# Attention of the second layer with its slots in another order on four engines: the fourth turned group is copied early, and each output is turned back and scaled within its own slot

## The reference, cut to what matters

```python
    def _L1_xattn_ref(hidden_states_query, hidden_states_key, attention_mask, Wq, bq, Wk, bk, Wv, bv):
        ...
        NUM_HEADS = 16
        HEAD_DIM = HIDDEN // NUM_HEADS
        ...
        q = _split_heads(hidden_states_query @ Wq.T + bq)
        k = _split_heads(hidden_states_key @ Wk.T + bk)
        v = _split_heads(hidden_states_key @ Wv.T + bv)
        scale = 1.0 / np.sqrt(HEAD_DIM)
        scores = jnp.einsum('bhqd,bhkd->bhqk', q * scale, k)
        scores = scores + ((1.0 - attention_mask) * -10000.0)[:, None, :, :]
        probs = jax.nn.softmax(scores, axis=-1)
        ctx = jnp.einsum('bhqk,bhkd->bhqd', probs, v)
        b, h, lq, d = ctx.shape
        return ctx.transpose(0, 2, 1, 3).reshape(b, lq, h * d)
```

## Time and profile before

| | |
|---|---|
| median of 3 runs | 851.43 us (850.89 to 852.59) |
| profiled execution, its time | 849.4 us |
| its span | 847.6 us |
| granted TensorE clock, mean | 0.984 |
| PE busy | 776.9 us (92%) |
| DVE busy | 506.0 us (60%) |
| ACT busy | 399.9 us (47%) |
| POOL busy | 227.0 us (27%) |
| the 15 slots from the first ACT copy of slot 1 to that of slot 16 | 489.22 to 614.81, 125.59 us |
| first `hidden` of the feed-forward that the attention no longer holds up (unit 1) | DVE at 632.29 |

### The profile page before, as it was taken

One profiled execution on the slowest core, in us unless ns is written; L12 is line 12 of the kernel. 1 busy time (PEld: TensorE's weight loads), 2 busy tenths in 40 slices (PEclk: granted clock), 3 DMA queues, 4 the chain that ended last, 5 costly groups with the idle time before them and its releaser, 6 DMA issues.

```text
span 847.6 us, 15310 instructions
## 1 busy us (share of the span) xinstructions
PE 776.9 (92%) x5406; PEld 625.7 (74%) x5406; DVE 506.0 (60%) x1159; ACT 399.9 (47%) x817; POOL 227.0 (27%) x208
## 2 busy tenths in 40 slices
PE   8667899999999999999999789996789999999997
PEld 7466487788887888888887455654568878888886
DVE  5588875465583333343342897978766665756644
ACT  5598554244462222222223688778635344243222
POOL 0079210046501332232234166764300000000000
PEclk9989999999999999999999999999999999999999
DMA  8478740033242334443332600102004023050140
GB/s 303 143 263 300 279 169 1 1 126 125 99 164 69 63 63 70 78 79 63 68 45 31 221 13 27 63 2 75 2 2 102 1 51 76 1 126 0 27 100 26
DMA packets 37512, 74.47 MB, mean 88 GB/s; under 512 B 4448, under 2 KB 25568, under 8 KB 35680
## 3 DMA queue, kind: packets, MB, share of 16 engines
q1 hardware_dynamic: 30288, 64.16, 24.0%
q0 software_dynamic: 7152, 9.34, 6.4%
HBM read 59.76 MB, written 19.01 MB: 93 GB/s over the span
## 4 chain that ended last, share of the span: by engine, by line
PE 54%; DVE 16%; ACT 8%; DVEq 4%; issue 4%; DMA 2%; ACTq 0%; POOLq 0%; SPq 0%
PE t_y_ps L2281 8%; PE f_y L1775 4%; PE a_turned L999 3%; PE a_score L977 2%; ACT a_hhi L1165 2%; PE t_gate L2251 2%; PE a_score L978 2%; PE a_score L979 2%; PE t_up L2262 2%; PE t_up L2263 2%; PE t_up L2261 2%; PE t_gate L2252 2%; PE t_gate L2253 2%; PE a_proj L876 2%; PE t_h_turned L2270 2%
## 5 line engine op out<-in xcount | busy, mean ns | idle before, releaser
L2221 POOL DMA_INDIRECT sums<-t_y,t_dest x39 | 60.9, 1561 | 168.4 <-DMA sums<-t_y,t_dest 81.3
L2316 ACT CAST t_xT_hi<-t_x_turned 128x256 fp32r<-128x256 f32 x39 | 14.5, 372 | 139.2 <-PE t_x_turned L2242 139.2
L2281 PE MATMUL t_y_ps<-W,t_hidT 128*128 x312 | 73.8, 379 | 0.8 <-ACT t_hidT L2326 0.8
L1165 ACT CAST a_hhi<-a_hid 128x512 fp32r<-128x512 f32 x48 | 29.8, 620 | 87.5 <-DVEq L1450 85.9
L2281 PEld LDWEIGHTS t_y_ps<-W,t_hidT 128*128 128x128 f32 x312 | 59.1, 190 | 10.5 <-issue 1.0
L1452 DVE TENSOR_TENSOR a_hlo<-a_hid,a_hhi 128x512 fp32r<-128x512 f32 x48 | 33.2, 693 | 35.1 <-ACT a_hhi L1165 35.1
L1154 ACT ACTIVATE a_act_g<-a_score 128x512 f32<-128x512 f32 x48 | 28.6, 596 | 46.4 <-PE a_score L979 45.9
L2345 DVE TENSOR_TENSOR t_hid<-t_act_g,t_up 128x512 f32<-128x512 f32 x39 | 28.5, 731 | 35.9 <-ACT t_act_g L2321 32.6
L832 POOL TENSOR_TENSOR a_sc<-a_sc,a_nmx 128x512 f32<-128x512 f32 x32 | 33.3, 1042 | 55.8 <-DVE a_nmx L1298 55.8
L1114 ACT ACTIVATE a_pr<-a_sc,a_nmx 128x128 f32<-128x128 f32 x128 | 40.8, 390 | 14.3 <-DVE a_nmx L1298 13.5
L2356 DVE TENSOR_SCALAR t_y<-t_y_ps,t_dest 128x256 f32<-128x256 f32 x39 | 18.9, 484 | 38.3 <-PE t_y_ps L2281 38.3
(11 more groups left out here) (426 smaller groups left out, 2287.8 us busy)
## 6 DMA issues: line engine op xcount, KB each, us to landing
W<-in_w_dram SPq DMA_DIRECT2D x9, 1536.0 KB, 8.1
a_cb<-comb_rows SPq DMA_DIRECT2D x16, 512.0 KB, 8.2
W<-m_rows SPq DMA_DIRECT2D x14, 512.0 KB, 4.9
slot_tokens<-in_blank_rows_dram SPq DMA_DIRECT2D x1, 5031.0 KB, 20.5
t_x<-slot_tokens SPq DMA_DIRECT2D x39, 129.0 KB, 3.0
a_raw<-in_w_dram SPq DMA_DIRECT2D x3, 1536.0 KB, 6.7
X<-in_x_dram SPq DMA_DIRECT2D x4, 512.0 KB, 6.1
ctxT_all<-in_ctxT_dram SPq DMA_DIRECT2D x4, 512.0 KB, 8.7
```

Of the source, the lines that this page charges most:

```text
L1165: act.copy(hhi[u % 2][:], hid[u % 2]).then_inc(hhi_ready, 1)
L2221: pool.indirect_dma_start(sum_dram, bass.IndirectOffsetOnAxis(ap=dest[p][:, 0:1].bitcast(U32), axis=0), y[p][:], None, compute_op=ALU.add) ...
L2281: last = pe.matmul(y_ps[p][:, 0:D], hidT[p][:, h], W[:, ds(e, 1), at:at + D], start=(h == 0), stop=(h == HT - 1))
```

## The change

It moves instructions and makes none new. `soft` is cut into `penalise` and `maxima`, so that something can stand between them. On PE, `turn_back(s-1)` comes behind `scores(s+1)` of the same slot instead of between the second and third `turn` of the next; `values(s-1, 3)` comes ahead of `scores(s+1)` instead of behind; the early projection comes behind `values(s-1, 1)` instead of ahead of `values(s-1, 0)`. On DVE, the copy of group 3 stands between the two halves of the scores, and `finish` stands at the slot's end, for sequence `s-1`; a late projection is copied one slot later, ahead of that copy. On ACT, `keep_out` stands between the two pairs of exponentials. On POOL, the addition to `X` stands behind the second `centre`.

```diff
@@ gpsimd
-            for s in range(B + 2):
+            for s in range(B + 1):
                 if s < B:
                     centre(s, 1)
-                if s >= 2:
-                    pool.wait_ge(o_ready, s - 1)
-                    pool.tensor_tensor(X[:, s - 2, :], X[:, s - 2, :], o_sb[s % 2][:], ALU.add).then_inc(added, 1)
                 pieces(s, 0)
                 if s < B:
                     centre(s, 3)
+                if s >= 1:
+                    pool.wait_ge(o_ready, s)
+                    pool.tensor_tensor(X[:, s - 1, :], X[:, s - 1, :], o_sb[(s - 1) % 2][:], ALU.add).then_inc(added, 1)
                 pieces(s, 1)
                 if s in (6, 11):
                     penalties(2 + (s == 11))
@@ tensor
                 if past:
                     turn(s - 1, 0)
                     turn(s - 1, 1)
-                if s >= 2:
-                    turn_back(s - 2)
-                if past:
                     turn(s - 1, 2)
                 if s == B:
                     gate_up(0)
-                if s == B + 1:
-                    break
-                if early:
-                    project(early)
                 if past:
                     values(s - 1, 0)
                     values(s - 1, 2)
                     turn(s - 1, 3)
                     values(s - 1, 1)
+                if early:
+                    project(early)
+                if s == B:
+                    gate_up(1)
+                if past:
+                    values(s - 1, 3)
                 if s + 1 < B:
                     scores(s + 1)
+                if 1 <= s < B:
+                    turn_back(s - 1)
                 if late:
                     project(late)
...
-                if past:
-                    values(s - 1, 3)
-                if s == B:
-                    gate_up(1)
...
                 down(u)
+                if u == 0:
+                    turn_back(B - 1)
@@ scalar
-                elif s == PREP0 + 1:
-                    normalise(0)
                 if s < B:
                     exps(s, 0)
                     exps(s, 1)
+                if s == PREP0 + 1:
+                    normalise(0)
                 keep(early)
+                if 1 <= s < B:
+                    keep_out(s - 1)
                 if s < B:
                     exps(s, 2)
                     exps(s, 3)
...
-                if s >= 1:
-                    keep_out(s - 1)
+                    keep_out(B - 1)
@@ vector
                 if s < B:
-                    soft(s, 0)
-                if s >= 2:
-                    finish(s - 2)
+                    penalise(s, 0)
+                    maxima(s, 0)
+                if past:
+                    keep(parts_of(s - 1)[1])
                 if s in (1, CH + 1):
                     normalise2(s // CH + 2)
-                if s < B:
-                    soft(s, 1)
-                keep(early)
-                if s == B:
-                    route_groups(0)
                 if past:
                     keep_turned(s - 1, 3)
                 if s == B - 1:
                     route_logits(0)
-                keep(late)
+                if s < B:
+                    penalise(s, 1)
+                if s in (PREP0 + 2, PREP0 + 3):
+                    keep_lo(0, s - PREP0 - 2)
+                if s < B:
+                    maxima(s, 1)
+                keep(early)
+                if 1 <= s < B:
+                    finish(s - 1)
...
-                elif s in (PREP0 + 1, PREP0 + 2):
-                    keep_lo(0, s - PREP0 - 1)
                 elif s == B:
+                    route_groups(0)
                     hidden(0)
+                    finish(B - 1)
                     route_second(0)
```

More of the change, by code:

```diff
@@ L1009, in _ @@
                 project(part)
-            for s in range(B + 2):
+            for s in range(B + 1):
                 early, late = parts_of(s)
-                past = 1 <= s <= B
+                past = s >= 1
                 if past:
@@ L1286, in normalise2, with penalise @@
                 last.then_inc(rows_dve, 1)
-            def soft(s, half):
+            def penalise(s, half):
                 c, j = s // CH, s % CH
@@ L1297, in soft, with maxima @@
                 dve.drain()
+            def maxima(s, half):
+                part = sc[s % 2][:, 2 * half:2 * half + 2].rearrange("p r i t -> p (r i) t")
                 dve.tensor_reduce(nmx[s % 2][:, 2 * half:2 * half + 2].rearrange("p r i -> p (r i)"), part, AX.X, ALU.max,
```

## The result

The changed kernel took 871.21 us (median of four runs, 867.34 to 874.5), against 851.17 us for the kernel before beside it (850.89 to 852.59). The ratio is 1.023, 95% interval 1.0181 to 1.028: slower by 20.0 us. The forecast was +14.2 us. The same program, timed again on another chip, gave 869.06 us against 850.58: ratio 1.0224 (1.0197 to 1.0251), +18.5 us. Direction and mechanism were right; the size was 4 to 6 us short. That it is slower is clear of the noise; whether by more than 2% is not, since both intervals hold 1.02.

A forecast was written before the change was run, and what follows sets the result against it. The prediction took a ring through four engines, closed by DVE's copy of group 3, to set slot lengths: +11.5 us in slots, +2.7 in the tail, 14.2 on 851.4, giving 865.6 us; 8-in-10 range 856 to 872.

The forecast's parts named there:

- What bounds the kernel: Attention before the change: PE near its limit only in early slots; a plain slot set by a 7.0 us cross-engine ring.
- the ring: Attention slots: DVE's copy of group 3 waits for PE's fourth turn, delaying penalty, maximum and exponentials; plain slot 8.0 us.
- The late slots: Slots 10 to 15: about break even, 54.7 us against 53.6, since their 2 us idle stretches go.
- 137.1: Slots 1 to 15: forecast slot lengths summed, in us, against 125.6 before, +11.5.
- I take +2.7: Tail, slot 16 to hidden(1): route_groups behind the copy and a wait at finish(15) delay hidden(1) by 2.7 us.
- K: Start of ACT's first copy in a slot, from which times count; the tail's hidden(0) was forecast 8.65 us after it.
- I carry the shift to the end at its full size: Behind the tail: PE busy nearly throughout in the same order, so the delay of hidden(1) reaches the end whole.
- the rival at 870 to 876 us: Early slots also drop to 1.2 GHz, about 1.4 us a slot in six slots, up to 8 us more; chance 13%.
- the ring's own, 858 to 870: Whole kernel: time range in us if the slots run as summed, 865.6 likeliest; chance 70%.
- the first rival: Slots: the copy of group 3 does not bind, 6.9 us a slot, about 844 us in all; chance 7%.
- PE does not hide it: Denies the rival that slots with projections stay at 8.7 us, PE covering late projections; 851 to 854 us, chance 10%.

The follow-up runs named there:

- e1: Changed kernel with the fourth turn ahead of the values of group 2 on PE; 865.59 us against 852.35 for the kernel before, ratio 1.0127.
- e6: Changed kernel with DVE's copy of group 3 moved behind the second penalty, still ahead of its maximum; 864.29 us against 869.06 for the plain changed kernel.
- e5: Changed kernel with extra identity transposes on PE filling idle stretches in slots 1 to 3 and 10 to 16; 868.2 us against 869.06 without them.
- e9: The kernel before, unchanged, profiled and timed again; 855.73 us against 854.12 for the same program in the same set, ratio 1.0023.
- e8: The changed kernel, unchanged, timed and profiled again on another chip; 869.06 us against 850.58 for the kernel before.
- e4: Changed kernel with DVE's order in slot 16 put back as before (route_groups ahead of the copy, finish(15) behind the routing); 868.93 us against 852.35, ratio 1.0163.
- e3: Kernel before with only DVE's copy of group 3 moved between the halves of the scores, behind finish(s-2); 888.52 us in one run.

## Why the prediction came out as it did

**What bounds the kernel, and the ring: right.** A plain slot took 7.95 (forecast 8.0), slots 2 and 3 took 8.46 and 8.47 (8.5), slot 4 took 9.68 (9.8), slot 5 took 10.17 (10.4), slots 6 and 7 took 8.48 (8.5), slots 8 and 9 as 4 and 5, slot 10 took 8.02 (8.0). e1 took wait from L1307, e6 put work into it, and slots 1 to 3 became shorter both times.

**The late slots: right within 1.2 us in all at the full clock.** In e5 slots 10 to 15 took 55.91 against 54.7 forecast; slot 11 was the term most off, 9.95 against 9.4. That the sum of all 15 slots comes within 0.3 us is better than its parts. The comparison with before has a flaw that could not be resolved: 137.1 is a sum at the full clock, 125.6 a measurement with a granted clock of 0.94 in its late slots, and neither profile of the kernel before had the full clock there. Slot 12 is the long one, as forecast: POOL's penalties stand behind the addition, which waits for `finish`. POOL, DVE and PE of the changed kernel there:

```profile
590.43 2.04 POOL L800 TENSOR_SCALAR a_pen<-a_pen 128x512 f32<-128x512 f32 x1
...
592.57 1.22 DVE L1295 TENSOR_TENSOR a_sc<-a_score,a_pen 128x1024 f32<-128x1024 f32 x1 [1.26 <-issue]
...
595.75 0.65 PE L915 MATMUL a_out_ps<-a_prT,a_v 128*32 128x128 f32 x8 [2.42 <-DVE a_prT L1307]
596.88 2.09 PE L891 MATMUL a_score<-a_kbd,a_qT 32*128 32x256 f32 x16 [0.48 <-DVE a_sc L1295]
```

DVE starts 0.1 us after the penalties end, the copy follows late, PE idles 2.42 us, and then the scores run at the 1.2 GHz level. The slot took 12.04 us (forecast 10.8), 10.93 with the clock held up.

**The tail: the mechanism was right, the term "I take +2.7" was too small.** It measured +4.6 us (two executions each). DVE and PE of the changed kernel, to be held against the earlier trace rows:

```profile
635.01 0.69 DVE L1307 COPY a_prT<-a_turned 128x512 f32<-128x512 f32 x1 [7.95 <-PE a_turned L903]
...
638.42 0.69 DVE L1442 TENSOR_TENSOR a_hid<-a_act_g,a_score 128x512 f32<-128x512 f32 x1
...
642.08 0.26 DVE L1313 RECIPROCAL a_rs<-a_out_ps 128x16 f32<-128x16 f32 x1 [1.55 <-PE a_out_ps L922]
...
650.27 0.68 DVE L1442 TENSOR_TENSOR a_hid<-a_act_g,a_score 128x512 f32<-128x512 f32 x1
...
634.32 0.66 PE L903 MATMUL a_turned<-cst,a_pr 128*128 128x128 f32 x4
...
```

Of the 2.8 us that `hidden(0)` loses at the full clock (K + 5.94 before in e9, K + 8.74 in e8), the prediction had 1.2. It forecast the new place well, K + 8.65, but took the difference from the old place in the profiled execution, K + 7.44, where the granted clock of the tail was 0.90. I put a forecast at the full clock against a measurement with the low clock in it. By the prediction's own figures the copy ends at K + 5.9, and that is where `hidden(0)` stood before at the full clock; so all 2.75 us of `route_groups` are new, not 1.2. From there to `hidden(1)` takes 11.87 us in e8 against 10.06 in e9, 1.8 more, where I had 1.3 to 1.5. The wait ahead of `finish(15)` is 1.56 us of it; `finish` itself is not, since it stood ahead of `hidden(1)` before too. Both parts together, 2.75 and 1.3, would have made the term about 4. In e4, with the old order in slot 16, the tail was back at 15.95 us. That the forecast place of `hidden(1)`, 20.2 us behind slot 16, lies only 0.4 from the 20.61 of e8 is luck: the low clock in the 17.48 that it starts from makes up for most of what the term lacks.

**"I carry the shift to the end at its full size": right.** The rest took 215.23 us against 215.31.

**The clock: the rival at 870 to 876 us was in part true.** The median of 871.21 lies in the rival's range and above the ring's own, 858 to 870; only the wider range, 856 to 872, holds it. The sum put the low clock at nothing. The profiled execution took 3.7 us more than the 863.6 forecast for it: the slots 1.5, of which 1.2 is the low clock by e5; the tail 1.8, of which 1.4 is the low clock (the fourth turn starts at K + 6.05, in e8 at K + 4.64); the later start of slot 1 0.4. The other 1.9 us of the median are its larger distance from the profiled execution, and no trace shows what they are; the two longest times came with the lowest granted clocks.

I asked whether gaps near 1 us would bring the low clock to the early slots. In the first profile they did not (1.00), in e8 they did in slot 3 (0.96 over nine slots), with the same program, and in e4 again in slot 3 with the same order there. The rule of the Trainium skill that I weighed ("TensorE: Matmul & The Clock Gate", section "Why this matters for your kernels") warns of long idle gaps. The trace of the first profile agrees with it in the early slots, that of e8 does not: the longest PE wait in slots 1 to 3 was 1.21 us, and the scores after it took 2.09 us. But one slot of nine fell, not the six of the rival, and the low clock cost 1.2, 1.6 and 4.9 us over all slots in the three profiles of this order, not 8.

**The other rivals** fell. The copy binds (14 waits where the first rival needs none), and PE does not hide it in the slots with projections: slot 4 took 9.68, not 8.7.

**In all: the mechanism was right, the sum too small.** The step that was most off is the tail's term, 2.7 where 4.6 us were measured (16.00 to 20.61 at clock 1.00 and 0.99). Besides it, the low clock, which the sum put at nothing, cost 1.2, 1.6 and 4.9 us of slots.

What is left over: the sum of the measured parts is +18.3 us, the medians say +20.0 and +18.5. With starts of slot 1 that differ by 5 us between executions of one program, and profiles that show the quicker executions of the changed kernel, the 0.2 to 1.7 us between are not to be resolved with two profiles each.

## What to carry to other kernels

In an engine that runs in order, an instruction that stands early may be worth less than the work behind it: ask when its input is ready by the rows, and put work that waits for nothing (here the second penalty, 1.2 us) ahead of it. Close the ring on paper from one cycle mark and check it at two places; that gave the lengths of slots 1 to 10 to within 0.25 us. And when a forecast at the full clock is set against a measured stretch, look up that stretch's granted clock first: here this one omission hid 1.5 us. Look also at where the profiled execution lies among the times: here it was the lowest of four, 3.9 us under their median.

## What the runs showed that I had not expected

- The same program gets the 1.2 GHz level in different slots in different executions: slot 3 took 8.47 us in one profile and 9.91 in another, slot 14 of the kernel before 10.65 and 8.93. The sum of the 15 slots of the changed order was 138.62, 139.01 and 142.28 us in three executions, so a single profile's sum may be off by some 4 us.
- The stages ahead of the attention, which no kernel here touches, end anywhere from 489.2 to 495.9 us, in the kernel before 489.22 and 494.14. What makes them vary was not tried.
- Moving one copy alone on one engine (e3, one execution, granted clock 0.94 and 0.82) cost 32 us in 15 slots, far more than its own 0.6 us in each.
